# Second mixture of experts in a four-layer gated block: gate and up products three units ahead of the down product instead of two, next pass's weights split one step sooner

## The reference, cut to what matters

```python
scores = jax.nn.softmax(x @ gate_w.T, axis=-1)
topk_ids, topk_w = _grouped_topk(scores)
combine = zeros.at[tokens, topk_ids].add(topk_w)        # (T, 8)
gu = jnp.einsum('th,eih->tei', x, w13_weight)           # (T, 8, 512)
gate, up = (gu[..., :INTER], gu[..., INTER:])           # INTER = 256
act = jax.nn.silu(gate) * up
act = act * combine[:, :, None]
out = jnp.einsum('tei,ehi->th', act, w2_weight)         # (T, 128)
```

## Time and profile before

| what | us |
|---|---|
| median of the runs | 377.65 |
| lowest and highest run | 376.38, 378.88 |
| profiled execution | 380.25 |
| its span, first to last instruction | 378.5 |
| TensorE busy in the span | 354.4 (94%) |
| VectorE busy | 280.2 (74%) |
| ScalarE busy | 213.2 (56%) |
| POOL (GpSimd) busy | 103.9 (27%) |

### The profile page before, as it was taken

The page is one execution under the profiler, slowest core; times in us unless marked ns, Lnnn a source line. Parts: engine busy times, 40 slices in busy tenths (PEclk is TensorE's granted clock), DMA queues, the critical chain, the costliest instruction groups (busy, mean ns, idle before and its releaser), DMA issues. The chain is left out here.

```text
span 378.5 us, 5695 instructions
## 1 busy us (share of the span) xinstructions
PE 354.4 (94%) x2020; PEld 266.4 (70%) x2034; DVE 280.2 (74%) x644; ACT 213.2 (56%) x389; POOL 103.9 (27%) x106
## 2 busy tenths in 40 slices
PE   6999989989999999989899999999989989999996
PEld 2667586857777888854688886667667646789765
DVE  5477978589776777786777769687767867788485
ACT  1315344567978889752466654767455514566382
POOL 6211751011344546220112101214556323000220
PEclk9999998999999999999999999999999998799999
DMA  6800120000474323000001100065350000000001
GB/s 192 291 3 0 51 66 5 4 5 4 132 217 158 90 76 82 5 0 2 0 2 43 42 2 0 0 189 163 97 167 2 0 2 0 0 3 2 0 2 55
DMA packets 18676, 20.37 MB, mean 54 GB/s; under 512 B 7119, under 2 KB 10729, under 8 KB 18649
## 3 DMA queue, kind: packets, MB, share of 16 engines
q1 hardware_dynamic: 18100, 19.52, 17.1%
q0 software_dynamic: 96, 0.32, 0.3%
q10 hardware_dynamic: 453, 0.18, 0.2%
HBM read 19.26 MB, written 0.59 MB: 52 GB/s over the span
## 5 line engine op out<-in xcount | busy, mean ns | idle before, releaser
L1229 DVE TENSOR_TENSOR rlo<-banks,rhi 128x512 fp32r<-128x512 f32 x64 | 44.0, 691 | 20.0 <-ACT rhi L744 19.1
L442 POOL TENSOR_TENSOR rstd<-var,neghalf 128x4 f32<-128x4 f32 x16 | 16.6, 1040 | 132.2 <-DVE var L918 132.2
L1436 PE MATMUL banks<-hhi,wuh 128*128 128x512 f32 x128 | 51.4, 402 | 0.6 <-DVE hlo L1128 0.5
L750 ACT ACTIVATE banks<-banks,b1s 128x512 f32<-128x512 f32 x64 | 42.4, 662 | 15.8 <-PE banks L1438 15.5
L1438 PE MATMUL banks<-hhi,wul 128*128 128x512 f32 x128 | 50.0, 391 | 0.0
L1437 PE MATMUL banks<-hlo,wuh 128*128 128x512 f32 x128 | 49.9, 390 | 0.0
L1436 PE MATMUL banks<-rhi,wdh 128*128 128x512 f32 x96 | 40.6, 423 | 8.2 <-DVE rlo L1229 3.4
L1443 PE MATMUL banks<-heat 128*128 128x512 bf16 x124 | 36.2, 408 | 4.1 <-POOL heat L420 2.9
L1847 PEld LDWEIGHTS banks<-vals,shared 128*128 128x128 f32 x320 | 37.7, 193 | 0.7 <-ACT shared L826 0.6
L826 ACT ACTIVATE shared<-banks 128x512 f32<-128x512 f32 (+1 forms) x48 | 23.7, 526 | 25.6 <-PE banks L1829 25.4
L1847 PE MATMUL banks<-vals,shared 128*128 128x27 f32 (+1 forms) x320 | 37.8, 271 | 0.1
(11 more groups left out here) (260 smaller groups left out, 708.8 us busy)
## 6 DMA issues: line engine op xcount, KB each, us to landing
rowB<-rowd SPq DMA_DIRECT2D x32, 256.0 KB, 4.3
up_raw<-in_w SPq DMA_DIRECT2D x8, 258.0 KB, 4.5
down_raw<-in_w SPq DMA_DIRECT2D x8, 256.0 KB, 5.1
up_raw<-in_v SPq DMA_DIRECT2D x8, 256.0 KB, 2.8
down_raw<-in_v SPq DMA_DIRECT2D x8, 128.0 KB, 3.4
mats<-in_mats SPq DMA_DIRECT2D x1, 640.0 KB, 5.5
mats<-in_mats SPq DMA_DIRECT2D x1, 576.0 KB, 4.1
x<-in_x SPq DMA_DIRECT2D x2, 256.0 KB, 3.6
```

Source lines behind the costliest of these rows:

```text
L750: nc.scalar.activation(bank[BANKS1[g % 4]][:, :], bank[BANKS1[g % 4]][:, :], ACT.Gelu, bias=b1s[p][:, c_:c_ + 1]).then_inc(q["gelu"], 1)
L1229: V.tensor_tensor(rlo[g % 4][:, :], bank[BANKS1[g % 4]][:, :], rhi[g % 4][:, :].bitcast(F32), ALU.subtract).then_inc(q["lo"], 1)
L1436: mm(o, lh, rh, start=start, stop=False)
```

## The change

TensorE makes gate and up products of unit g + 3 instead of g + 2 before the down product of g. ScalarE splits the next pass's up weights in other steps: for p = 0 in step 3 instead of 4 (in the first pass still 4), for p = 1 in step 5 instead of 6. On POOL the low half for p = 0 is made before the sum of group 4i instead of after it. LAG2 is used only in TensorE's loop.

```diff
-        LAG1, LAG2 = 3, 3
+        LAG1, LAG2 = 3, 4
...
-                add(4 * i, "r", r)
                 if i < LAST:
                     split_up(i + 1, 0, r)
+                add(4 * i, "r", r)
                 add(4 * i + 1, "r", r)
                 if i < LAST:
                     split_up(i + 1, 1, r)
...
                 if n == 1 and i > 0:
                     down_hi(i, 1, N2, C2, r)
-                if n == 4 and i < LAST:
+                if n == (4 if i == 0 else 3) and i < LAST:
                     up_hi(i + 1, 0, 1, N2, r, r["u"])
-                if n == 6 and i < LAST:
+                if n == 5 and i < LAST:
                     up_hi(i + 1, 1, 1, N2, r, r["u"])
                 if n == 7 and i < LAST:
                     down_hi(i + 1, 0, N2, C2, r)
```

## The result

| | before | after |
|---|---|---|
| median of 16 runs each, us | 378.44 | 381.06 |
| ratio, with its 95% interval | | 1.0071 (1.0041 to 1.0101) |
| span of the profiled execution | 378.5 | 379.7 |
| first matmul of gate 5 | 237.07 | 237.60 |
| first matmul of down 31 | 302.73 | 305.92 |

What follows compares the result with a forecast made beforehand. TensorE's queue was taken to bound the second mixture: -6.5 us of waits removed and +9.2 of new stalls give +2.7, so 380.3 us against the median of 377.65. Range 375.5 to 384.0.

Steps and rivals of the forecast that it cites:

- What bounds the stage: Second mixture, 81.8 us: TensorE's queue, busy for 76.9, sets its length; only TensorE's idle time can be won.
- What the lead removes: Second mixture: TensorE's waits for low halves before down products go, except 0.3 at down 18; 6.5 us gained.
- What it adds: Second mixture: gates wait for silu behind early weight splits, the router's weights and at the head; 9.2 us lost.
- router's copy: ScalarE's L729 in steps 7 and 11, ahead of silu 9 and 13: delays gates 10 and 14, 1.54 us each.
- the load: Third pass's weights on SP, wanted by step 3 of pass 2: land in time, cost 0; a third slower, 1.1 us.
- The end: Down 31: up 31 comes 0.68 us earlier, what hangs on transposes L1745 comes 0.68 later behind it; 0.
- The queues passed: POOL's moved split and SP's transfers cost nothing; VectorE's first weighing may stand for 0.8 us, covered at down 10.
- the ledger of before: TensorE's losses before down products in the kernel before: 2.3, 2.1 and 2.4 us, together 6.8.
- ScalarE being late anyway: ScalarE reaches the early splits after their wait is over, so they cost 0; 371.8 us, chance 0.09.
- VectorE's lateness staying: Down products in the routing stretch and down 16 still wait for VectorE, 3.3 us more; 383.6 us, chance 0.10.
- Nothing: Gains and new waits cancel; 377.7 us, chance 0.08 together with the clock's faster end.
- The clock: Another clock fall in the mixture, 383.3 us, chance 0.07; or the present one at 320 to 330 us absent, 377.3.

Runs made afterwards that it cites:

- experiment 2: Kernel before with TensorE's lead of three units and POOL's new order, up weights split in the old steps; ratio 0.9891, gate 5 to down 31 61.95 us.
- experiment 7: The kernel before, unchanged, profiled a second time; one execution of 378.28 us, span 376.5, gate 5 to down 31 65.66 us again.
- experiment 4: Two kernels, each the changed kernel with one split put back: p=1 in step 6 (377.23 us), or p=0 in step 4 (379.15 us).
- experiment 6: Changed kernel with old split steps, router's copy behind silu, POOL's keys behind pass 2's sums, rlo 31 before x's update; 372.16 us, 0.9840 against kernel before.

## Why the prediction was right, point by point

**What bounds the stage.** Right. TensorE's order and its waits made the difference: the ledger below closes on 2.66 us to within 0.1.

**What the lead removes (forecast 6.5).** In the stretch all rlo waits but down 31's went; under 1 us was forecast for them, 0.88 is left. Down 18 kept 0.34 + 0.10 (forecast 0.3). PE's timeline of the kernel after:

```profile
278.92 0.50 PE L1436 MATMUL banks<-rhi,wdh 128*128 128x512 f32 x1 [0.18 <-POOL wdl L467]
```

**What it adds (forecast 9.2).** Lateness against 0.227 a matmul, with the slow first matmul, in the kernel after:

| ahead of | forecast | measured | cause |
|---|---|---|---|
| gate 7 | 0.4 | 0.35 | no down in between |
| gate 8 | 1.9 | 1.89 | split in step 5, output |
| gate 10 | 1.54 | 1.57 | router's copy |
| gate 12 | 0.2 | 0.20 | weights, rhi, output |
| gate 14 | 1.54 | 1.51 | router's copy, split hidden |
| gate 16 | 1.35 | 1.40 | split in step 5 |
| gate 22 | 0.95 | 1.48 | split in step 3, and the load |
| gate 24 | 1.35 | 1.40 | split in step 5 |
| sum | 9.2 | 9.8 | |

The router's copy (gate 14) in the kernel after, PE and ACT:

```profile
259.59 0.60 PE L1723 MATMUL banks<-const,c 128*8 128x128 f32 x4
...
260.23 0.59 ACT L729 ACTIVATE cT<-banks 8x512 f32<-8x512 f32 x1
260.72 0.57 ACT L846 ACTIVATE shared<-banks 128x512 f32<-128x512 f32 x1
```

0.64 from transposes to copy (0.63 in the earlier trace rows) and 0.49 to silu (0.5 taken). Of the "some seven" waits for silu, 1.1 to 1.8 each, the trace marks six, of 1.15 to 1.65.

**The step that was mis-sized: the load.** Gate 22 was forecast with a load that lands 0.2 before it's wanted, with 1.1 as the other end. ScalarE's copy and the queue of transfers in the kernel after:

```profile
275.57 0.43 SPq L331 DMA_DIRECT2D down_raw<-in_v  x1
...
279.42 0.63 ACT L603 ACTIVATE wuh<-up_raw 128x512 fp32r<-128x512 f32 x1 [2.77 <-DMA down_raw<-in_v]
```

The copy starts 3.85 after the issue, not 3.3. By up 21, whose last matmul starts at 278.35, it could have started at 278.83: 0.6 was lost, of which 0.5 shows at gate 22. The 3.3 that the forecast took was the median of two transfers, the third pass's and the one behind it. The third pass's own took 3.8 already in the kernel before, as its transfers of 268 to 274 us alone show (KB, us from issue to landing):

```profile
down_raw<-in_v SPq DMA_DIRECT2D x1, 128.0 KB, 3.8
```

So the size was in the trace, and the median hid it, in a place without slack.

**The end (forecast 0).** Down 31 starts 3.76 after up 31's last matmul (302.16), before 3.23; less the 0.68 of the moved down that is -0.15. VectorE waited 0.44 for the transposes, as said.

**The queues passed (forecast 0).** POOL's order: experiment 2, 0.01 us. VectorE's first weighing waited 0.9 for the router's row, as said (0.8), and down 10, behind it, wasn't held.

**Total.** 9.8 new, plus 0.44 at down 18, less 6.8, less 0.15 is 3.3; measured are 2.66. The missing 0.6 is what the ledger of before left out: down 5 started 0.16 late with a first matmul slower by 0.11, and three first matmuls, behind the router's transposes and at down 8, were slower by 0.08 each, 0.5 in all; 0.1 wasn't traced. So the mechanism and seven of the eight prices were right within 0.1, but that the sum hit 2.7 so exactly is luck: two errors of half a microsecond, in the load and in the ledger of before, cancelled.

**The rivals.** ScalarE being late anyway: fell, it was idle 1.8 to 2.8 us ahead of each of the five early splits. VectorE's lateness staying: fell, see the waits. Nothing: fell, the ratio's interval leaves out 1. The clock: the part "the present fall may not come" did come true for the profiled execution, whose span is only 1.2 us longer. But experiment 7 shows that the place of the falls changes from one execution to the next of the same kernel, so the missing fall can't be put down to the change; the timed medians, +2.6 and a ratio of 1.0071, go with the stretch and not with the span.

## What to carry to other kernels

A longer lead on one engine moves what the next engine must have done first: write down, for the new order, which instruction of the helper's program releases each product of the leader, and what stands ahead of it there. A filler instruction that waits for product X must not stand ahead of the one that frees the bank for the product behind X; it is free only behind it, where the helper would be idle. Here the lead was worth 3.7 us and "one step sooner" for its fillers cost 6.4. Both follow from the order of the instructions and a few durations read from the trace; and a change in two parts should be timed in its parts. Where an order leaves no slack, read the one transfer that it hangs on, not the median of several.

## What the runs showed of the hardware that was not expected

The granted clock falls to its lower level (0.50, 1.2 GHz) for some microseconds in nine of the ten profiled executions ahead of 360 us, at places that differ for the same kernel. The kernel before had it at 50 to 60 us in both profiles (0.83 over ten us) and at 320 to 330 in one of the two (0.70). The kernel after had it at 220 to 230 (0.83), where all engines still do the same as before; both kernels of experiment 4 and that of experiment 6 had one there too, and the kernel before in neither profile. In the first profile the fall of 320 to 330 us cost 2.0 us between down 31 and the first matmuls behind the transposes at the second attention's end (302.73 to 355.74, against 305.92 to 356.93), as much as most of what was to be measured.

TensorE was idle 1.08 us before the fall at 56 us. But it was idle as long at the same place in the kernel after, which kept 1.00 over all of 50 to 60 us; PE's timeline of the kernel before, then of the kernel after:

```profile
56.25 1.15 PE L1449 MATMUL banks<-const,h 128*128 128x128 f32 x4 [1.08 <-DVE h L925]
...
55.39 1.01 PE L1449 MATMUL banks<-const,h 128*128 128x128 f32 x4 [1.07 <-DVE h L925]
```

The gaps of 1.15 to 1.65 us in the mixture of the kernel after were followed by no fall either. What decides it stays open.

A matmul of 512 columns of the mixtures came every 0.227 us in quiet stretches. The Trainium skill, "TensorE: Matmul & The Clock Gate", section "Back-to-back issue gap", gives 216 ns for an isolated warm one, and no product of the mixture comes that fast in any of the runs. The filler `keep_busy`, of 512 columns too but in bf16, does. PE's timeline of the kernel before, at clock 1.00:

```profile
310.48 3.63 PE L1443 MATMUL banks<-heat 128*128 128x512 bf16 x16
...
315.00 0.38 PE L1443 MATMUL banks<-heat 128*128 128x512 bf16 x1 [0.16 <-issue]
```

Sixteen take 3.63 and one takes 0.38, so they came every (3.63 - 0.38) / 15 = 0.217 us. Whether the operands' type makes the 0.010 between the two wasn't tested.
